# A five-stage transformer kernel: fp4 rounding step from a scaled absolute value, normalizations on ScalarE, gamma and row decay folded into other operands

## The reference

```python
x = x + 0.5 * ffn_fp4(LN(x))           # f0, f = 0..7
x = x + retention(LN(x))               # a0
x = x + 0.5 * ffn_fp4(LN(x))           # f0, f = 8..15
x = x + 0.5 * soft_moe(LN(x))          # f1, j = 0..7
x = x + attention_lora(LN(x))          # a1
x = x + 0.5 * soft_moe(LN(x))          # f1, j = 8..15

def fp4_quant_dequant(x):              # blocks of 16 along the last dim
    scale = max(max|xb| / 6, 1e-12);  xn = xb / scale
    q = GRID[searchsorted(MID, |xn|)] * sign(xn) * scale
    # GRID 0 .5 1 1.5 2 3 4 6
def ffn_fp4(x):                        # hidden width 704
    h = silu(Q(x) @ Q(w_gate).T) * (Q(x) @ Q(w_up).T);  return Q(h) @ Q(w_down).T
def retention(x):                      # blocks of 128 tokens, decay .99
    v = x @ Wv * .01;  k = sigmoid(x @ Wk + bk);  q = sigmoid(x @ Wq + bq)
    a = (q @ k.T) * decays;  y = a @ v + (q @ kv_state) * decays[:, :1];  return y @ Wo
def soft_moe(x):                       # 1024 slots, gelu MLP of 1024
    xn = rms_norm(x) * gamma_x;  se = rms_norm(slot_embeds) * gamma_slot
    logits = xn @ se.T
    slots = softmax_over_experts(logits).T @ xn
    out = softmax_over_slots(logits) @ (gelu(slots @ w1) @ w2)
```

## Time and profile before

| | us |
|---|---|
| median of 3 runs | 2934.41 |
| lowest, highest | 2932.08, 2935.42 |
| the profiled execution | 2929.66 |
| its span | 2927.6 |
| TensorE busy | 2429.8 (83%) |
| VectorE busy | 2108.1 (72%) |
| ScalarE busy | 1625.4 (56%) |
| GpSimd busy | 1096.1 (37%) |

### The profile page before, as it was taken

The page is one execution under the profiler, slowest core; times in us unless marked ns, Lnnn a source line. Parts: engine busy times, 40 slices in busy tenths (PEclk is TensorE's granted clock), DMA queues, the critical chain, the costliest instruction groups (busy, mean ns, idle before and its releaser), DMA issues.

```text
span 2927.6 us, 56018 instructions
## 1 busy us (share of the span) xinstructions
PE 2429.8 (83%) x23228; PEld 1846.8 (63%) x23228; DVE 2108.1 (72%) x3530; ACT 1625.4 (56%) x2761; POOL 1096.1 (37%) x791
## 2 busy tenths in 40 slices
PE   1677777778888988889889889889898888898888
PEld 0445555555666766657567666667666667677666
DVE  6599999889898886777877777776786765343432
ACT  2244544454765757365566556574656566556554
POOL 0144544444352443244443526262525252222112
PEclk9799998899999999989898999999989999999999
DMA  4000000000000000000000000000000000000000
GB/s 153 17 1 1 1 1 1 1 1 1 1 1 1 1 1 1 23 13 12 11 14 2 23 2 23 2 23 2 23 9 21 12 2 8 8 8 1 8 8 8
DMA packets 34572, 32.96 MB, mean 11 GB/s; under 512 B 7377, under 2 KB 33681, under 8 KB 34321
## 3 DMA queue, kind: packets, MB, share of 16 engines
q1 hardware_dynamic: 34320, 29.40, 3.1%
HBM read 12.34 MB, written 4.19 MB: 6 GB/s over the span
## 4 chain that ended last, share of the span: by engine, by line
PE 44%; DVE 17%; ACT 6%; issue 4%; POOL 4%; SPq 1%; DMA 1%; POOLq 0%; DVEq 0%; ACTq 0%
PE psum L623 11%; PE psum L625 10%; PE psum L624 10%; PE psum L629 3%; PE psum L1055 2%; DVE a1pr L1771 2%; PE psum L1057 2%; PE psum L1056 2%; POOL f1hT L2042 2%; PE psum L906 1%; PE psum L959 1%; DVE f1d L1882 1%; DVE a1c L1789 1%; PE psum L936 1%; DVE f1e L1886 1%
## 5 line engine op out<-in xcount | busy, mean ns | idle before, releaser
L2042 POOL TENSOR_TENSOR f1hT<-f1g,f1hT 128x512 f16<-128x512 f32 x256 | 311.7, 1224 | 677.1 <-ACT f1hT L1422 676.6
L2029 POOL TENSOR_TENSOR a1pr<-a1PT,a1pr 128x1024 f16<-128x1024 f32 (+1 forms) x176 | 350.3, 1992 | 334.9 <-DVE a1pr L1771 334.9
L623 PE MATMUL psum<-f1sl,f1w1h 128*128 128x256 f16 x1024 | 290.4, 284 | 30.7 <-DVE f1pr L1929 16.6
L623 PE MATMUL psum<-f1w2h,f1hT 128*128 128x256 f16 x1024 | 282.4, 276 | 17.0 <-POOL f1hT L2042 15.2
L624 PE MATMUL psum<-f1sl,f1w1h 128*128 128x256 f16 x1024 | 290.0, 283 | 0.0
L625 PE MATMUL psum<-f1sl,f1w1l 128*128 128x256 f16 x1024 | 289.7, 283 | 0.0
L624 PE MATMUL psum<-f1w2l,f1hT 128*128 128x256 f16 x1024 | 281.6, 275 | 0.0
L625 PE MATMUL psum<-f1w2h,f1hT 128*128 128x256 f16 x1024 | 281.4, 275 | 0.0
L1748 DVE TENSOR_REDUCE a1nm<-psum 128x2 f32<-128x768 f32 (+3 forms) x176 | 198.1, 1125 | 79.1 <-PE psum L886 77.7
L2006 POOL TENSOR_TENSOR f0hT<-f0Y,f0hT 128x512 f16<-128x512 f32 (+1 forms) x128 | 139.6, 1105 | 181.4 <-ACT f0Y L1214 181.4
L1771 DVE CAST a1pr<-a1PT 128x1024 f16<-128x1024 f32 (+1 forms) x176 | 156.0, 891 | 69.5 <-ACT a1PT L1318 49.5
(11 more groups left out here) (335 smaller groups left out, 7502.1 us busy)
## 6 DMA issues: line engine op xcount, KB each, us to landing
a1Q<-a1st SPq DMA_DIRECT2D x96, 64.0 KB, 2.6
a1K<-a1st SPq DMA_DIRECT2D x96, 64.0 KB, 2.5
x<-in_L_attn_x SPq DMA_DIRECT2D x8, 512.0 KB, 8.8
out<-x SPq DMA_DIRECT2D x8, 512.0 KB, 3.0
wslot<-in_L_ffn_w SPq DMA_DIRECT2D x1, 1024.0 KB, 7.5
wraw<-in_L_ffn_w SPq DMA_DIRECT2D x1, 1024.0 KB, 5.7
wslot<-in_L_ffn_slot_embeds SPq DMA_DIRECT2D x1, 1024.0 KB, 8.2
a1Q<-a1mr SPq DMA_DIRECT2D x64, 4.0 KB, 1.7
```

The lines of the kernel that those rows point to most:

```text
L623: e.matmul(out, lh, rh, start=start, stop=False)
L2029: e.tensor_tensor(a1["pr"][:, i % 2, 1, :, 0:w], a1["PT"][:, i % 2, :, 0:w], a1["pr"][:, i % 2, 0, :, 0:w], ALU.subtract).then_inc(s["a1_pl"])
L2042: e.tensor_tensor(hT1[:, 1, 2 * hp:2 * hp + 2, :], gg[:, hp % 2, :, :], hT1[:, 0, 2 * hp:2 * hp + 2, :], ALU.subtract).then_inc(s["f1_hl"])
```

## The change

The magic number becomes 2^23/1.9. ScalarE computes M = |MAGIC * Y| straight from Y, and the two VectorE steps take max(M, MAGIC) in place of M + MAGIC; the bit masks go. The layernorm's product for f0, a0 and a1 becomes ScalarE's Identity with scale rstd and bias -mean * rstd; for the bias VectorE negates the means and GpSimd multiplies them by rstd. f1 keeps it on VectorE. gamma_x is folded into w1's rows and into the slot embeddings, and a second copy of it, two columns, is loaded. The row decay of q goes into the per-row factor of a0's output (C_OUT); QS becomes the scale of the Copy. Some scales change with it (AS, SS, YS). Semaphores are renamed to match. `Rehearsal` is unchanged.

```diff
@@ -17,12 +17,12 @@
 WS, XS, HS = 64.0, 64.0, 16.0
-QS, AS, VS, SS, YS = 1024.0, 64.0, 256.0, 16.0, 16.0
+QS, AS, VS, SS, YS = 1024.0, 16.0, 256.0, 4.0, 4.0
 SLS, VA = 16.0, 16.0
 BETA = DECAY ** P
-C_ID, C_ROW, C_MASK, C_VB, C_MAG, C_BF = 0, 128, 256, 384, 385, 386
+C_ID, C_MASK, C_VB, C_OUT, C_BF = 0, 128, 256, 257, 258
 C_ALL = C_BF + 288
-MAGIC = 1.5 * 2.0 ** 22
+MAGIC = 2.0 ** 23 / 1.9
 TIE = 1.0 - 2.0 ** -22
...
@@ -567,10 +567,12 @@
                 e.dma_start(gx[:, :], a["L1_ffn_gamma_x"].partition_broadcast(P)).then_inc(s["w_dma2"], 16)
+                e.dma_start(g1[:, :], a["L1_ffn_gamma_x"].rearrange("(k p) -> p k", p=P),
+                            allow_slow_non_contiguous=True).then_inc(s["w_dma2"], 16)
                 e.dma_start(raw_w1.rearrange("p (k n) -> p k n", k=2),
                             a["L1_ffn_w1"].rearrange("(k p) n -> p k n", p=P)).then_inc(s["w_dma2"], 16)
                 yield 45.0
-                q.wait_ge("w_dma2", 144)
+                q.wait_ge("w_dma2", 160)
                 q.wait_ge("w_T", W_N["down", 3])
...
@@ -1140,14 +1142,18 @@
 
+            def scaled(c, b, out, t):
+                st, mv, ve, rstd = ln[c]
+                return e.activation(out, xb[:, b, t, :], ACT.Identity, bias=rstd[:, 1, t:t + 1], scale=rstd[:, 0, t:t + 1])
+
             def weights():
                 yield 0.0
                 q.wait_ge("w_dma", 96)
                 for i, (key, n) in enumerate((("gate", 1280), ("up", 1280), ("tail", 512), ("down", 1408))):
                     yield (5.0, 12.0, 19.0, 28.0)[i]
-                    m2 = wM[0:64 if key == "tail" else P, 0:n]
-                    q.wait_ge("w_qm", i + 1)
-                    e.activation(m2, m2, ACT.Relu, scale=MAGIC, bias=cst[0:m2.shape[0], C_MAG:C_MAG + 1]).then_inc(s["w_qr"])
+                    rows = slice(0, 64 if key == "tail" else P)
+                    q.wait_ge("w_qy", i + 1)
+                    e.activation(wM[rows, 0:n], wY[rows, 0:n], ACT.Abs, scale=MAGIC).then_inc(s["w_qr"])
 
...
@@ -1163,18 +1169,27 @@
                     yield 44.0 + 2.0 * i
-                    q.wait_ge("w_dma2", 176 if key == "w2" else 144)
+                    q.wait_ge("w_dma2", 192 if key == "w2" else 160)
                     src, dst = raw_split(key)
-                    e.activation(dst[0], src, ACT.Copy, scale=WS).then_inc(s["w_sh"])
+                    if key == "w1":
+                        q.wait_ge("w_g", 1)
+                        for k in range(2):
+                            e.activation(dst[0][:, k, :], src[:, k, :], ACT.Copy, scale=g1[:, k:k + 1]).then_inc(s["w_sh"])
+                    else:
+                        e.activation(dst[0], src, ACT.Copy, scale=WS).then_inc(s["w_sh"])
 
             def f0_tokens(f):
                 S = at_f0(f)
                 for tp in range(2):
                     n = 2 * f + tp
+                    yield S + 2.0 + 20.0 * tp
+                    q.wait_ge("ln_rs", 2 * (f + 1))
+                    q.wait_ge("f0_xT", n)
+                    for i in range(2):
+                        scaled("x", f % B, f0["xh"][:, i, :], 2 * tp + i).then_inc(s["f0_xn"])
                     yield S + 4.0 + 20.0 * tp
-                    q.wait_ge("w_dma", 96)
                     q.wait_ge("f0_xm", n + 1)
-                    e.activation(f0["Mx"][:, :], f0["Mx"][:, :], ACT.Relu, scale=MAGIC, bias=cst[:, C_MAG:C_MAG + 1]).then_inc(s["f0_xr"])
+                    e.activation(f0["Mx"][:, :], f0["Yx"][:, :], ACT.Abs, scale=MAGIC).then_inc(s["f0_xr"])
                     yield S + 7.8 + 20.0 * tp
...
@@ -1193,10 +1208,9 @@
                                  scale=1.0 / (XS * WS)).then_inc(s["f0_si"])
-                    yield G + 8.0
+                    yield G + 7.2
                     q.wait_ge("f0_hm", ft + 1)
-                    m2 = f0["M"][:, t % 2, :]
-                    e.activation(m2, m2, ACT.Relu, scale=MAGIC, bias=cst[:, C_MAG:C_MAG + 1]).then_inc(s["f0_hr"])
+                    e.activation(f0["M"][:, t % 2, :], f0["Y"][:, t % 2, 0:F], ACT.Abs, scale=MAGIC).then_inc(s["f0_hr"])
 
...
@@ -1215,6 +1229,11 @@
                 S = at_a0(b)
+                yield S + 2.0
+                q.wait_ge("a0_rs", 2 * (b + 1))
+                q.wait_ge("a0_xu", 4 * b)
+                for t in range(NT):
+                    scaled("a", b, a0["xh"][:, t, :], t).then_inc(s["a0_xn"])
                 for k in range(2):
...
@@ -1233,8 +1252,8 @@
                         yield S + 9.4 + 1.5 * g
-                        q.wait_ge("a0_qr", 2 * b + c + 1)
-                        e.activation(a0["qT"][:, 0, c, :], a0["qf"][:, c, :], ACT.Copy).then_inc(s["a0_qh"])
+                        q.wait_ge("a0_sg", 4 * b + c + 1)
+                        e.activation(a0["qT"][:, 0, c, :], a0["qf"][:, c, :], ACT.Copy, scale=QS).then_inc(s["a0_qh"])
                     else:
...
@@ -1485,13 +1508,24 @@
                     yield 45.0 + 2.0 * i
-                    q.wait_ge("w_sh", i + 1)
                     src, dst = raw_split(key)
-                    e.scalar_tensor_tensor(dst[1], src, WS, dst[0], ALU.mult, ALU.subtract).then_inc(s["w_sl"])
+                    if key == "w1":
+                        q.wait_ge("w_sh", i + 2)
+                        for k in range(2):
+                            ins = e.scalar_tensor_tensor(dst[1][:, k, :], src[:, k, :], g1[:, k:k + 1], dst[0][:, k, :], ALU.mult, ALU.subtract)
+                    else:
+                        q.wait_ge("w_sh", i + 1 + (i > W_SPLIT["w1"] - 1))
+                        ins = e.scalar_tensor_tensor(dst[1], src, WS, dst[0], ALU.mult, ALU.subtract)
+                    ins.then_inc(s["w_sl"])
 
             def slot_weights():
+                yield 33.0
+                q.wait_ge("w_dma2", 160)
+                e.tensor_scalar(g1[:, :], g1[:, :], WS, None, ALU.mult).then_inc(s["w_g"])
+                e.tensor_tensor(gslot, gslot, gx[:, :], ALU.mult).then_inc(s["dve"])
+                q.tick()
                 yield 40.0
-                q.wait_ge("w_dma2", 176)
+                q.wait_ge("w_dma2", 192)
                 e.memset(wst[:, 112:120], 0.5).then_inc(s["dve"])
...
@@ -1530,11 +1564,10 @@
                 q.wait_ge("dve", k)
+                if c != "p":
+                    e.tensor_scalar(ve[:, 1, :], mv[:, :, 0], -1.0, None, ALU.mult).then_inc(s["dve"])
+                    q.wait_ge("dve", q.tick())
                 e.tensor_scalar(ve[:, 0, :], mv[:, :, 1], 1e-5, None, ALU.add).then_inc(s[up_to])
-
-            def scaled(c, b, out, t, row):
-                st, mv, ve, rstd = ln[c]
-                return e.tensor_scalar(out, xb[:, b, t, :], mv[:, t, 0:1], rstd[:, row, t:t + 1], ALU.subtract, ALU.mult)
 
...
@@ -1544,19 +1577,15 @@
                     q.wait_ge("a0_xu", 4 * b + 4)
+                q.wait_ge("f0_xn", 4 * f)
                 normalize("x", b, "ln_ve")
                 xh, Yx, Mx = f0["xh"], f0["Yx"][:, :], f0["Mx"][:, :]
                 v = xh[:, :, :].rearrange("p t d -> p (t d)")
                 c_, r_ = f0["scx"][:, 0, :], f0["scx"][:, 1, :]
                 for tp in range(2):
                     n = 2 * f + tp
-                    yield S + 2.0 + 20.0 * tp
-                    q.wait_ge("ln_rs", f + 1)
-                    q.wait_ge("f0_xT", n)
-                    for i in range(2):
-                        scaled("x", b, xh[:, i, :], 2 * tp + i, 0).then_inc(s["dve"])
-                        k = q.tick()
-                    q.wait_ge("dve", k)
+                    yield S + 2.8 + 20.0 * tp
+                    q.wait_ge("f0_xn", 2 * n + 2)
                     q.wait_ge("f0_xq", n)
...
@@ -1564,14 +1593,12 @@
                     q.wait_ge("dve", q.tick())
-                    e.scalar_tensor_tensor(blocks16(Yx), blocks16(v), -TIE, bc(r_, 16), ALU.mult, ALU.mult).then_inc(s["dve"])
-                    q.wait_ge("dve", q.tick())
-                    e.tensor_scalar(Mx.bitcast(u32), Yx.bitcast(u32), 0x7F800000, None, ALU.bitwise_and).then_inc(s["f0_xm"])
+                    e.scalar_tensor_tensor(blocks16(Yx), blocks16(v), -TIE, bc(r_, 16), ALU.mult, ALU.mult).then_inc(s["f0_xm"])
                     yield S + 4.6 + 20.0 * tp
                     q.wait_ge("f0_xr", n + 1)
-                    e.scalar_tensor_tensor(Yx, Mx, MAGIC, Yx, ALU.add, ALU.add).then_inc(s["dve"])
+                    e.scalar_tensor_tensor(Yx, Mx, MAGIC, Yx, ALU.max, ALU.add).then_inc(s["dve"])
                     q.wait_ge("dve", q.tick())
-                    e.scalar_tensor_tensor(Yx, Mx, MAGIC, Yx, ALU.add, ALU.subtract).then_inc(s["f0_xy"])
+                    e.scalar_tensor_tensor(Yx, Mx, MAGIC, Yx, ALU.max, ALU.subtract).then_inc(s["f0_xy"])
                     yield S + 8.4 + 20.0 * tp
...
@@ -1602,18 +1629,14 @@
                     q.wait_ge("dve", q.tick())
-                    e.scalar_tensor_tensor(blocks16(Y), blocks16(h), -TIE, bc(r_, 16), ALU.mult, ALU.mult).then_inc(s["dve"])
```

(43 more changed lines are left out.)

40 lines of the change are left out of this document (20 added, 20 removed), and 4 rows, old and new, of the table s.

## The result

The changed kernel takes **2862.65 us** (median of 4 runs, 2861.58 to 2865.14) against 2933.24 for the kernel before beside it (2931.53 to 2935.42): ratio 0.9767 [0.9756, 0.9779], 70.6 us less. Forecast were 2864 us, a range of 2810 to 2920, and 0.88 for faster. The profiled execution has a span of 2861.2 us.

What follows compares the result with a forecast made beforehand. VectorE was taken to set the pace in B, VectorE and TensorE both in C. The stage terms -42 - 15 - 3 - 7 - 3 = -70 gave 2859.7, forecast as 2864 us at the runs' median; range 2810 to 2920.

Steps and rivals of the forecast that it cites:

- Rival 4: ScalarE: Abs and Identity do need table loads of 1.28 us; +53 us, 2987 us; chance 0.02.
- B, -42: Stage 179 to 707 us, eight a0 beside some eight f0: VectorE's relief shortens it by 42 us (bounds -62 and -10).
- +1.4 us for each front: Start of each a0: negation, product, Identities and a hop lengthen the normalization's path by 1.4 us (bounds +0.5 and +3.1).
- C, -15: Stage 707 to 1159 us, rest of f0 beside the first f1: 15 us shorter (bounds -35 and +5).
- The charge, 5 us: Rehearsal's 1283 ns per change to Abs or Identity, in the plan only; some 5 us of stage B's gain left out.
- Rival 3: Planned order queues each of 96 Abs behind ScalarE's copies, VectorE's rounding waits: slower, +28 us, 2962 us; chance 0.06.
- The relief per microsecond, 57%: Stage B: some 57% of the relief taken as gain, because the lane's own latency doesn't shrink with the load.
- Rival 1: Full relief: every step of the a0 and f0 lanes waited for VectorE's queue; -122 us, 2812 us; chance 0.17.
- the 88%: TensorE's busy share in stages C and D, taken as a limit on how far VectorE's relief can shorten a stage.
- A, -3: Start-up, to 179 us: weights' mask and other VectorE pieces go, a small DMA is added; -3 us (bounds -10 and +5).
- D -3 and E -7: a1 beside f1 (1159 to 2431 us), then the last f1 alone: normalization moved, gamma product removed; -3 and -7 us.
- Rival 2: The a0 and f0 lanes' latency holds, only on-path pieces go: -25 us, 2909 us; chance 0.16.

Runs made afterwards that it cites:

- e1: The changed kernel with Abs and Identity counted as free of a table load in the rehearsal (order only): 2819.5 us, 0.9615.
- e6: The kernel before with only the normalizations of f0, a0 and a1 moved to ScalarE's Identity, counted as free in the rehearsal: 2875.73 us, 0.9809.
- e12: e1 with VectorE's signal lag in the rehearsal 160 ns, not 120 (order only): 2787.18 us, 0.9505.
- e3: The kernel before with the fp4 rounding alone changed, the rehearsal charging Abs 1283 ns for a change of function: 2888.29 us, 0.9851.
- e4: The changed kernel, same queue order, with 96 exponent masks of f0 put back on VectorE, output unused, hidden from the rehearsal: 2904.03 us, 0.9909.
- e5: The kernel before with the fp4 rounding alone changed, Abs counted as free in the rehearsal: 2877.8 us, 0.9816.
- e11: e1 with ScalarE's signal lag in the rehearsal 200 ns, not 160 (order only): 2817.21 us, 0.9607.
- e2: The kernel before with Relu charged as a table of its own in the rehearsal (order only): 2907.0 us, 0.9920.
- e7: The kernel before with only gamma folded into w1 and the slot embeddings: 2903.78 us, 0.9908.
- e8: The kernel before with only the row decay of q folded into a0's output factor: 2923.33 us, 0.9970.
- e9: The kernel before with ScalarE's signal lag in the rehearsal 200 ns, not 160 (order only): 2935.17 us, 1.0017.
- e10: The kernel before with VectorE's signal lag in the rehearsal 160 ns, not 120 (order only): 2936.95 us, 1.0021.

## Why the prediction was right, and where only its sum was

The total, 2864 against 2862.65, rests on errors that cancel. By the prediction's own steps:

**The instruction costs held.** Abs 0.793 and 0.632 us (0.79, 0.63), Identity 0.591 to 0.599 (0.58), the negation 0.18 for f0 and 0.44 for a0 (0.22), loads 159 (near 151). The product on GpSimd took 0.26 to 0.32 in mean where I chose 0.5 between 0 and 1.006. L1650's change of form cost (1.032 - 0.912) x 16 = 1.9 us where I took 0. Rival 4 (table loads) is refuted: no load stands ahead of 96 Abs and 128 Identities. The trace agrees with the rule that the prediction cites from the Trainium skill ("ScalarE: Activation LUTs", "Table sets: the hidden batching unit"), that identity and abs stand in every set.

**B, -42: measured -40.4, and in part luck.** Only 22 us of it are idle time of TensorE; the other 18 are its busy time, and 66 matmuls fewer lie in the stage. The last a0 update came at 645.9 instead of 662 only because A ended 20 us early. VectorE's share is 86%, TensorE's 80% (forecast 84). And B is so near only with the charge in it: uncharged it takes 473.1 us, -54 (e1).

The wait for a0kT shrank from 17.5 to 4.5 us, as forecast, but the one for a0xh shrank too, from 19.0 to 3.2, where I had it grow. Part of that only changed its name: the wait for a0xT, the next step of the same front, grew from 3.1 to 14.9, so both together went from 22.1 to 18.1 us (16.1 in e1). The step "+1.4 us for each front" held for the chain itself: from the first statistics to the last Identity it takes 7.9 us in after and 7.4 in e1, where the last normalized tile came after 5.7 before (means of eight, from the times in the traces).

What I overlooked is a wait that the change moves (it is in the diff). In before a0(b)'s statistics wait on VectorE for a0(b-1)'s last update of x; in after only ScalarE's Identities do. In before that update (L1698) came later than f0's in all seven pairs, so the whole front stood behind it:

```profile
437.18 0.41 DVE L1698 SCALAR_TENSOR_TENSOR x<-psum,x 128x256 f32<-128x256 f32 x1
...
437.95 1.40 DVE L1526 BATCH_NORM_STATS2 lnsta<-x 128x6 f32<-128x256 f32 x4
...
441.66 1.38 DVE L1537 TENSOR_SCALAR a0xh<-x,lnmva,lnrsa 128x256 f32<-128x256 f32 x4 [0.90 <-POOL lnrsa L1954]
```

In e1 the statistics run ahead of it (first VectorE, then ScalarE):

```profile
454.55 1.39 DVE L1560 BATCH_NORM_STATS2 lnsta<-x 128x6 f32<-128x256 f32 x4
...
459.75 0.48 DVE L1712 SCALAR_TENSOR_TENSOR x<-psum,cst,x 128x256 f32<-128x256 f32 x1 [0.26 <-PE psum L627]
```

```profile
460.33 2.08 ACT L1147 ACTIVATE a0xh<-x,lnrsa 128x256 f32<-128x256 f32 x4 [3.54 <-DVE x L1712]
```

From the later of the two updates of x to the last normalized tile it takes 6.05 us in before, 5.39 in after, 4.22 in e6, 3.19 in e1 and 3.01 in e12 (means of seven). In after f0's update is the later one in four of seven, and then the full front follows it. How much of the gain is this shorter path and how much VectorE's relief isn't shown: no run moves the wait alone.

**C, -15: measured +16.8 by length.** A part is the boundary: C took over 140 matmuls, and TensorE's busy time there rose by 20 us. TensorE's idle time fell by 3.5 us only; in e1 it fell by 15. So the relief that I forecast for C is there in the uncharged order and all but missing in the charged one.

**The charge, 5 us: the mis-sized term.** "I have left some 5 us of gain in B out for it" was the one price on which everything hung: between after and e1 it is 43 us, and 53 in B and C. Rival 3's mechanism is there, at a third of its 123 us; rival 3 as a whole, slower than before, isn't. I said that VectorE's waits for the Abs would grow to tens of microseconds. The group of VectorE that waits for the 704-wide step, whole span, before and then after:

```profile
L1612 DVE SCALAR_TENSOR_TENSOR f0Y<-f0M,f0Y 128x704 f32<-128x704 f32 x64 | 60.1, 938 | 11.6 <-ACT f0M L1199 11.4
```

```profile
L1635 DVE SCALAR_TENSOR_TENSOR f0Y<-f0M,f0Y 128x704 f32<-128x704 f32 x64 | 62.8, 981 | 7.2 <-ACT f0M L1213 7.1
```

VectorE's idle time for it fell from 11.4 to 7.1 us, but the Abs did come late, as rival 3 has it; VectorE was merely given other work meanwhile. One case in after, VectorE and then ScalarE:

```profile
481.03 0.89 DVE L1632 SCALAR_TENSOR_TENSOR f0Y<-f0h,f0sc 128x704 f32<-128x704 f32 x1
...
490.30 0.88 DVE L1635 SCALAR_TENSOR_TENSOR f0Y<-f0M,f0Y 128x704 f32<-128x704 f32 x1
```

```profile
481.44 1.14 ACT L1256 ACTIVATE a0qT<-a0qf 128x512 f16<-128x512 f32 x2
...
489.11 0.77 ACT L1213 ACTIVATE f0M<-f0Y 128x704 f32<-128x704 f32 x1
```

Y is ready at 481.92; sigmoids and copies of a0 and f0 go first, and the Abs starts 7.2 us later. In the mean of the 64 hidden tiles the Abs starts 2.8 us after its Y in after and 0.6 in e1, and the rounding step on VectorE starts 1.5 us after the Abs has ended, 1.0 in e1 (from the times in the traces). From Y to Abs it is 3.3 us in e3 and 2.7 in e4, both charged, and 0.5 to 0.7 in e5, e11 and e12, uncharged; from Y over the mask to Relu it is 1.7 in before and 3.7 in e2, the charged one. TensorE's waits at L625 for f0h from VectorE over B and C are 17.4 us in after and 8.2 in e1 (7.9 at L623 in before); with all its other waits for f0h the sums are 22, 19 and 28 us, so that wait alone doesn't carry the difference.

**The relief per microsecond, 57%: too low.** With VectorE's busy totals from each profile:

| kernel | VectorE less, us | time less, us | ratio |
|---|---|---|---|
| e3 rounding, charged | 63.7 | 43 | 0.68 |
| e5 rounding | 72.8 | 56 | 0.77 |
| e6 normalization | 64.9 | 58 | 0.89 |
| e7 gamma | 45.1 | 30 | 0.67 |
| e8 row decay | 14.7 | 10.5 | 0.71 |
| e1 all | 163.9 | 112 | 0.68 |
| e12 all | 175.5 | 144 | 0.82 |
| e4, at a fixed order | 45.7 | 41.4 | 0.91 |
| after | 155.0 | 70.6 | 0.46 |

Rows of before are subtracted from (2108.1 us), for e4 the row of after (1953.1). I had 47 + 74 = 121 us removed in B and C and took 57, which is 0.47. The ratios are rough: these totals hold more than the instructions that left. Orders of before with no instruction changed (e2, e9, e10) lie 10 to 17 us below it, so e8's row says nothing, and e7's 45.1 us are 23.9 of work, which would make its ratio 1.26. Only e4's keeps one order. Rival 1, 2812 us, is near what uncharged orders bring (2819.5, 2817.2), and I gave it 0.17. And the 88% that I took as TensorE's ceiling in C is none: it reached 91% there in e1 (391 of 430) and 92% in e12 (394 of 426).

**A, -3: measured -20.5, the step that failed most.** I looked only for instructions that leave A. The timeline of ScalarE in after, and of VectorE in before, e2 and e1, where f0(0)'s input gets its statistics:

```profile
37.51 1.09 ACT L1147 ACTIVATE f0xh<-x,lnrsx 128x256 f32<-128x256 f32 x2 [0.61 <-POOL lnrsx L1967]
```

```profile
61.76 1.41 DVE L1526 BATCH_NORM_STATS2 lnstx<-x 128x6 f32<-128x256 f32 x4
```

```profile
31.93 1.40 DVE L1526 BATCH_NORM_STATS2 lnstx<-x 128x6 f32<-128x256 f32 x4
```

```profile
58.37 1.40 DVE L1560 BATCH_NORM_STATS2 lnstx<-x 128x6 f32<-128x256 f32 x4
```

x's first tiles wait for nothing but the order: in before they stand behind the preparation of the weights until 61.8 us. In the charged orders (after, e2 to e4) they go at 32 to 34 us, in all the uncharged at 55 to 62; A takes 159 to 165 us in the first and 165.5 to 181 in the second. Order alone gives 14 us (e2), the instructions with an uncharged order 12 (e1; 8 in e11, 14 in e12). So the same charge that goes with 53 us more in B and C brings a good start. The charge on the rounding is enough for it (A 160.4 us in e3, 173.0 in e5); by which of its steps wasn't tried.

**D -3 and E -7: measured -31 and +8.6, together -22.** Gamma in E came out as forecast in after: the spacing of the last four f1 updates sums to 391.6 us after 398.9, 1.8 us each (forecast about 2). The order moves this number as much, though: it is 397 to 406 in e2, e9 and e10 and 385 with gamma alone (e7). The gamma product is gone from these groups of VectorE in stage E, which answer to the earlier trace rows:

```profile
L1841 DVE TENSOR_SCALAR f1u<-x,lnmvp,lnrsp 128x256 f32<-128x256 f32 x16 | 5.6, 410 | 1.6 <-PE psum L631 1.5
...
L1849 DVE TENSOR_TENSOR f1xnl<-f1u,f1xnh 128x1024 f16<-128x1024 f32 x4 | 5.0, 1252 | 2.5 <-ACT f1xnh L1371 2.5
```

E is longer by the 105 matmuls that it took over from D (+12 us busy), D shorter by 167 (-14 at 85 ns) and by shorter ones, 84.6 ns each against 85.5; idle time fell by 5 in D and 3 in E. "D keeps its length within 1%" was wrong as a test, since D's length isn't a measure of work. e2 and e5, which change no instruction in D and E, have 28 and 17 us less there; e9 and e10 have 11 and 8 more. Those stages move by -28 to +11 us with the order, and the change's own share in them can't be told from it by these runs.

**Rival 2** (the lanes' latency holds, 2909) fell with its reason: TensorE waited 4 us less at a0's front in all, not longer.

So the total was right by cancellation. By length A gave 17 us more than forecast and D with E 12 more, B 2 less and C 32 less.

## What to carry to other kernels

Where a planner writes each engine's order from a table of costs, a change of function names can alter the order more than it alters the work: run the new work under the old costs and the old work under the new ones, and each in more than one order, before crediting either. When work moves to another engine, ask also what its wait moves: here everything that stood behind the wait in the old queue, the statistics and the power, was free to run early. Compare time from input to output, not the duration of the two instructions. Compare stages by idle time of the bounding engine, not by length, once their boundaries can take work from each other.

## What the runs showed of the hardware

- One instruction on VectorE has no fixed length. L1668 took 684 ns where the same instruction took 1239 before, and a mask of 704 elements 626 to 804 ns by stage and 527 ns in A of e4. Of the 64 such masks of before, the 19 with GpSimd busy during more than half of their time took 1173 ns in mean, the other 45 522 (from the times in the trace); that GpSimd is the cause isn't shown by a run that changes it alone. Busy totals of unchanged instructions move with the schedule: e12 has the instructions of after and 20.5 us less of VectorE.
- TensorE's own busy time is a term of the sum. The granted clock of a profile is the mean over stretches at its two levels, 2.4 and 1.2 GHz. The same 23228 matmuls took 2429.8 us at a granted clock of 0.935, 2420.5 at 0.942, 2392.5 at 0.955 (e1) and 2381.0 at 0.956 (e12). Of e1's 116 us of span 37 are this, 79 are idle time. In B and C the clock was 0.98 in e1, with 121 us of TensorE idle, and 0.95 before with 171; but in e2 it was 0.93 with 168, so the sum of idle time doesn't set it alone.
- A table load took 1283 ns in all kernels, and the order alone moved their number between 151 and 165 (before, e2, e9, e10), 14 x 1.28 = 18 us of ScalarE.
